# A three-block window-attention kernel: input turning and table preparation in one stage, parameter loads on two queues

## What is computed

```python
xn   = layernorm(x) * g1 + b1
q, k, v = split(window_partition(roll(xn)) @ qkv_w + qkv_b)
attn = softmax(q @ k.T * 8**-0.5 + rel_table[rel_index] + shift_mask)
x    = x + roll_back(window_reverse(attn @ v @ proj_w + proj_b))
x    = x + gelu((layernorm(x) * g2 + b2) @ w1 + c1) @ w2 + c2
```

## Time and profile before

| what | value |
|---|---|
| median of three runs | 7142.31 us (7137.75 to 7150.61) |
| profiled execution | 7153.04 us, of it 7151.3 us span |
| PE, DVE, ACT, POOL busy over the span | 96%, 46%, 63%, 31% |
| last `evac_cm` of the input turning | 175.0 us |
| DVE starts to clear `V3` | 317.9 us |
| DMA share of the first and last fortieth of the span | 8 and 7 tenths, 0 between |

### The profile page before, as it was taken

How to read it: one execution, slowest core, us unless ns; L and a number is a source line. 1 busy time by engine, 2 the same in 40 slices (tenths; PEclk the granted TensorE clock), 3 DMA queues, 4 the chain that set the end, 5 groups by cost and what they waited for, 6 DMA issues and landing times.

```text
span 7151.3 us, 325290 instructions
## 1 busy us (share of the span) xinstructions
PE 6879.3 (96%) x141786; PEld 4832.6 (68%) x141786; DVE 3312.7 (46%) x6694; ACT 4473.2 (63%) x6933; POOL 2233.0 (31%) x2070
## 2 busy tenths in 40 slices
PE   6599999999999999999999999999999999999997
PEld 4277676777677777776777677777776777677764
DVE  6444444444444444444444444444444444444444
ACT  0166666666666666666666666666666666666660
POOL 4033333333333333333333333333333333333330
PEclk9699999999999999999999999999999999999995
DMA  8000000000000000000000000000000000000007
GB/s 246 22 19 24 23 25 23 23 24 23 23 24 23 23 24 23 25 23 23 25 23 24 24 23 24 24 23 25 23 25 23 23 25 23 23 23 25 23 19 236
DMA packets 291287, 244.34 MB, mean 34 GB/s; under 512 B 45888, under 2 KB 285474, under 8 KB 289570
## 3 DMA queue, kind: packets, MB, share of 16 engines
q1 hardware_dynamic: 245238, 180.65, 9.4%
q10 hardware_dynamic: 36414, 19.95, 0.9%
q0 software_dynamic: 8192, 22.49, 0.9%
HBM read 113.42 MB, written 109.53 MB: 31 GB/s over the span
## 4 chain that ended last, share of the span: by engine, by line
PE 93%; DMA 3%; issue 2%; DVE 1%; SPq 0%; POOL 0%; ACT 0%; POOLq 0%; DVEq 0%; ACTq 0%
PE pS L959 14%; PE pA L1001 14%; PE pS L972 9%; PE pA L922 7%; PE pB L1010 6%; PE pS L981 6%; PE pB L1058 5%; PE pA L1050 5%; PE pB L1041 4%; PE pB L1079 4%; PE pB L1098 4%; PE pA L928 4%; PE pA L1089 3%; PE pB L1018 3%; PE pB L1106 3%; PE pA L1018 2%
## 5 line engine op out<-in xcount | busy, mean ns | idle before, releaser
L461 POOL TENSOR_TENSOR Kbd<-KT,headmask 128x588 f32<-128x588 f32 x768 | 895.5, 1166 | 3358.1 <-DVE KT L740 3358.1
L729 DVE TENSOR_REDUCE mx<-pS 113x12 f32<-113x588 f32 x1536 | 1181.0, 769 | 1259.2 <-PE pS L981 1253.5
L959 PE MATMUL pS<-bias,stackr 128*128 128x296 f32 x6096 | 1334.6, 341 | 3.6 <-ACT E L531 3.3
L531 ACT ACTIVATE E<-pS 113x588 f32<-113x588 f32 x1536 | 1004.8, 654 | 451.2 <-DVE mx L729 420.3
L461 POOL TENSOR_TENSOR Qbd<-Qt,headmask 128x588 f32<-128x588 f32 x768 | 895.9, 1167 | 1068.6 <-DVE Qt L734 1068.6
L959 PEld LDWEIGHTS pS<-bias,stackr 128*128 128x128 f32 x6096 | 932.3, 189 | 328.3 <-issue 227.3
L1001 PEld LDWEIGHTS pA<-E,V 113*54 113x54 f32 x36864 | 962.0, 131 | 112.3 <-issue 111.9
L1001 PE MATMUL pA<-E,V 113*54 113x49 f32 x36864 | 1010.8, 215 | 1.1 <-ACT va L520 0.8
L515 ACT ACTIVATE sq<-pB 112x392 f32<-112x392 f32 x768 | 381.8, 497 | 789.7 <-PE pB L1010 789.7
L972 PE MATMUL pS<-Kbd,Qt 24*49 24x147 f32 x24576 | 765.7, 304 | 0.0
L981 PE MATMUL pS<-Qbd,KT 27*49 27x147 f32 x24576 | 707.0, 285 | 0.0
(11 more groups left out here) (126 smaller groups left out, 9085.4 us busy)
## 6 DMA issues: line engine op xcount, KB each, us to landing
xin<-xT SPq DMA_DIRECT2D x384, 98.0 KB, 2.0
xT<-xout SPq DMA_DIRECT2D x384, 98.0 KB, 1.9
xin<-xT SPq DMA_DIRECT2D x384, 73.5 KB, 2.0
xT<-xout SPq DMA_DIRECT2D x384, 73.5 KB, 1.8
xT<-cm POOLq DMA_DIRECT2D x128, 171.5 KB, 3.7
cm<-xT SPq DMA_DIRECT2D x128, 171.5 KB, 3.4
tm<-in_x SPq DMA_DIRECT2D x128, 147.0 KB
out<-tm ACTq DMA_DIRECT2D x128, 147.0 KB
```

What stands on the lines that cost most here:

```text
L461: return pool.tensor_tensor(y, x, m, ALU.mult)
L531: act.activation(e, s, ACT.Exp).then_inc(exp_done, 1)
L729: dve.tensor_reduce(m, s, AX.X, ALU.max).then_inc(mx_done, 1)
L959: mm(pS[:, q, S1:S1 + 2 * SW], stackr[:, :], rows, start=True, stop=False)
```

## The change

On every engine the 128 turning steps are now written out, without loops. On DVE and PE a counter `turned` and two helpers, `turn(n)` and `turn_to(step)`, place them between the instructions of the preparation:

- DVE: one step behind each of the three one-hot instructions, behind each pair of `neg`, behind each group of six mask additions, behind `high`, behind each `bias` pair, and behind the scaling of each block's weights. The waits for `whole` stand at step 48 (block 0), 90 (block 1) and 100 (block 2). The second index's one-hot tiles are made at step 32, before the first `bias`.
- PE: the first gather begins at step 10 with one step behind each matmul (20 matmuls, steps 10 to 30), the second at step 38 with two steps behind each (steps 38 to 78). The bias matmuls come at step 110, the centring at the end. The centring uses banks 2, 3 and 7 in place of 0, 1 and 2.
- Queues: ACT loads the six table pieces first (a semaphore of their own, `tab_in`), then 28 parameters. It now issues the store of `gath` and the loads of `whole`. Another 28 parameters are issued by ACT between the second store of `gath` and the wait for it. The other 97 parameters are issued by SP, one behind each tile load from step 4 on. SP loads the second index behind the tile of step 20.
- POOL: the same 128 stores, written out.

The core of the diff:

```diff
+        BY_ACT = 56
 (SP)
             load_index(0)
-            for c in range(4, UN):
+            sp.wait_ge(zeroed, len(CLEARED) + 1)
+            for c in range(4, STEPS):
                 load_x(Step(0, c))
-            with sp.Fori(1, STEPS // UN) as u:
...
+                if c - 4 < len(par) - BY_ACT:
+                    to, of = par[BY_ACT + c - 4]
+                    sp.dma_start(to, of).then_inc(par_in, 16)
+                if c == 20:
+                    sp.wait_ge(onehot, 1)
+                    load_index(1)
 (ACT)
-            for to, of in par:
+            for to, of in tabs:
+                act.dma_start(to, of).then_inc(tab_in, 16)
+            for to, of in par[0:BY_ACT // 2]:
                 act.dma_start(to, of).then_inc(par_in, 16)
...
+                act.wait_ge(gat_done, 10 * (k + 1))
+                act.dma_start(gat[k, 0:kept], gath[rows]).then_inc(gat_out, 16)
+                if k:
+                    for to, of in par[BY_ACT // 2:BY_ACT]:
+                        act.dma_start(to, of).then_inc(par_in, 16)
+                act.wait_ge(gat_out, 16 * (k + 1))
+                for t in ts_:
+                    if t:
+                        act.wait_ge(whole_used, t)
...
 (DVE)
+            def turn_to(step):
+                while turned[0] < min(step, STEPS):
+                    c = turned[0]
+                    spread_x(Step(0, c))
+                    if c:
+                        evac_cm(Step(0, c - 1))
+                    turned[0] += 1
...
+            turn(4)
+            one_hot(0)
...
+            turn_to(32)
+            one_hot(1)
             for k, (_, ts_) in enumerate(TABLES):
...
                 for t in ts_:
+                    turn_to((48, 90, 100)[t])
                     dve.wait_ge(whole_in, 128 * (t + 1))
...
 (PE)
+            turn_to(10)
+            pe.wait_ge(tab_in, 16 * len(tabs))
...
+                turn_to((10, 38)[k])
                 pe.wait_ge(onehot, k + 1)
...
                         mm(o, tab[:, 0, heads], ..., start=True, stop=False)
+                        turn(1 + k)
                         mm(o, tab[:, 1, heads], ..., start=False, stop=True).then_inc(gat_mm, 1)
+                        turn(1 + k)
+            turn_to(110)
+            pe.wait_ge(par_in, 16 * len(par))
```

More of the change, by code:

```diff
@@ L204, in build @@
         const_in = sem("const_in")
-        par_in = sem("par_in")
+        par_in, tab_in = sem("par_in"), sem("tab_in")
         idx_in = sem("idx_in")
@@ L629, in evac_cm, with turn, one_hot @@
                 dve.tensor_copy(strided(cm[:, b, 0:1], [[TK, TP], [1, TK]]), src).then_inc(cm_done, 1)
-            dve.wait_ge(zeroed, 1)
[L632 to L640, removed]
+            turned = [0]
+            def turn_to(step):
[5 more added lines that the diff above has]
+                    turned[0] += 1
+            def turn(n=1):
+                turn_to(turned[0] + n)
+            def one_hot(k):
+                dve.wait_ge(idx_in, 16 * (k + 1))
+                chain(dve.tensor_copy(idx_f[:, :], idx_i[:, :]))
+                turn()
+                if k:
+                    dve.wait_ge(gat_mm, 10)
+                dve.tensor_scalar(oh_lo[:, :], idx_f[:, :], kcol[:, 0:1], None, ALU.is_equal)
+                turn()
+                dve.tensor_scalar(oh_hi[:, :], idx_f[:, :], kcol[:, 1:2], None, ALU.is_equal).then_inc(onehot, 1)
+                turn()
+            dve.wait_ge(zeroed, 1)
+            turn(4)
             dve.wait_ge(zeroed, len(CLEARED) + 1)
@@ L868, in transpose_x, with turn_to, turn @@
                 last.then_inc(tr_done, 1)
-            for c in range(UN):
-                transpose_x(Step(0, c))
-            with pe.Fori(1, STEPS // UN) as u:
-                for c in range(UN):
-                    transpose_x(Step(u, c))
-            pe.wait_ge(cm_done, STEPS)
-            pe.wait_ge(par_in, 16 * len(par))
+            turned = [0]
+            def turn_to(step):
+                while turned[0] < min(step, STEPS):
+                    transpose_x(Step(0, turned[0]))
+                    turned[0] += 1
+            def turn(n=1):
+                turn_to(turned[0] + n)
+            turn_to(10)
+            pe.wait_ge(tab_in, 16 * len(tabs))
+            pe.wait_ge(zeroed, len(CLEARED) + 1)
             g = 0
             for k, (_, ts_) in enumerate(TABLES):
+                turn_to((10, 38)[k])
                 pe.wait_ge(onehot, k + 1)
```

59 lines of the change are left out of this document (24 added, 35 removed).

## The result

| | before | after |
|---|---|---|
| median of four runs each | 7140.78 us (7137.75 to 7150.61) | 7061.51 us (7058.22 to 7062.18) |
| ratio, 95% interval | | 0.9886 (0.9869 to 0.9903) |
| last turning copy (`evac_cm`) starts | 175.0 us | 228.1 us |
| DVE starts to clear `V3` | 317.9 us | 239.0 us |
| from there to the first copy of the output turning | 6682.0 us | 6669.0 us |

The kernel is 79.3 us faster by the medians. The forecast was 77 us and 7065 us. The head alone is shorter by 78.9 us. The two profiled executions differ by 92 us, and the other 13 us lie in the pipeline, whose code is the same. They belong for the most part to the profiled execution of before: in the twelve experiments the pipeline, whose code is the same in all, took 6664 to 6677 us.

The account below looks back on a forecast made before the run. PE bounds the pipeline, which stays unchanged; only the head can move. Terms of +54.7 us on the turning put the clearing of `V3` at 240.7 us instead of 317.9, 77 us less: 7065 us, range 7050 to 7081.

Parts of the forecast that it names:

- The range: Whole kernel: gain of 61 to 92 us from the bounds of single terms; total 7050 to 7081 us, elsewhere 7085.
- The ring of stores: Turning of the input: a ring of four `cm` buffers takes 5.2 us, which sets 1.30 us a step.
- I put it at zero: Turning loops written out on every engine: takes some register instructions away, counted as no gain.
- Step 3: First gather, turning steps 10 to 30, PE sets the pace: 40 us against 26, +14 us (+10 to +24).
- Steps 6 and 10: Masks, `high` and `bias` of blocks 0 and 2, turning steps 48 to 65 and 100 to 117: +10.3 us each.
- Step 7: Turning steps 65 to 77, PE sets the pace: 1.57 us a step, +3.2 us (0 to 5).
- Step 8: New DVE wait for `whole` at turning step 90, behind 28 parameter issues on ACT: +3.6 us (0 to 8).
- Step 11: Bias matmuls at PE's turning step 110, where DVE sets the pace: +1 us (0 to 3).
- Held tile loads: Rival: parameter loads in SP's queue hold the tile loads behind them; 17 us slower, 7159 us, chance 0.04.
- Slow gathers: Rival: in the gathers PE stays at 1.2 GHz and strided passes double to 1.74 us; 7110 us, chance 0.16.
- Full cover: Rival: the turning catches up at once, DVE's own work is the floor; gain 118 us, 7024 us, chance 0.14.
- Starved stores: Rival: woven DVE instructions make POOL's stores of `cm` 3.5 us late; +9.5 us, 7075 us, chance 0.08.

Follow-up runs that it names:

- e3: The kernel before with the 128 turning steps written out on SP, DVE, PE and POOL, nothing woven: 7132.47 us, ratio 0.9988.
- e11: The kernel before with the 128 turning steps written out on SP, DVE, PE and POOL, run once more: 7135.10 us, ratio 0.9986.
- e5: The changed kernel with ACT's second 28 parameter loads moved behind block 1's loads of `whole`: clearing of `V3` at 236.1 us, 2.9 us earlier.
- e2: The kernel before with only the division of the loads, 97 of them on SP behind tile loads, nothing woven: 7140.47 us, ratio 1.000.
- e6: The changed kernel with the second index loaded in seven pieces behind tile loads 16 to 22: clearing of `V3` at 237.1 us, 1.9 us earlier.

## Why the prediction was right, and where it was not

The sum came within 2 us of the head (78.9 against 77), but by terms that erred both ways. The mechanism held, each stretch as long as its slowest engine or wait makes it; that the number came so close is in part luck. In the sum block 0's stretch was 3.7 us too long and the second gather's 3.5, the way to `high` of block 1 was 5.8 us too short and the bias matmuls 2.2.

- **What bounds the kernel.** Right. Nothing behind the clearing of `V3` changed.
- **The range.** Its bounds were added up wrongly. With all the bounds named at one end together, the gain is 54 to 98 us, not 61 to 92. The measured 78.9 lies in both. The upper end of the total also reads 7081 us in one place and 7085 in another.
- **The ring of stores.** Right as the pace of the plain turning. But 1.30 us a step was the pace of the looped turning; written out it is 1.23 and 1.22 (`e3`, `e11`). "I put it at zero" is the one term that failed outright: it is worth 9 to 10 us when the turning is not woven. What of it is in the 79 us is open.
- **Step 3, the first gather.** 40 us forecast, 40.0 measured, by two errors. `way` 0 went faster, since PE, without a gap, stays at the higher clock (14.8 us against 17). In `way` 1, "the load of the second index hides" was wrong: it held stores for 5.1 us and a tile for 1.1 us.
- **Steps 6 and 10, `bias`.** Mechanism right, DVE full. The size was off: 28.7 us against 32.4, because the turning's two copies overlap and cost 0.74 us, not 0.92. Counting mean durations of back-to-back instructions counts the overlap twice. The rows had shown it: from 9.4 to 177.2 us DVE is busy 108.24 us, while 128 steps of 0.92 us make 118. The prediction's DVE share of 170 us up to 318 us is such a sum too; the busy time of that window is 161 us. In step 10 the 3.2 us of step 11 filled the gap.
- **Step 7.** 15.3 us against 18.8: PE was full, at the higher clock, two steps in 2.64 us.
- **Step 8, the new wait.** Right in place and cause (`e5` removes it), 6.2 us against 3.6, inside its bounds. The 28 issues took 16.6 us, with one pair of 3.6 us among them. The turning steps ahead of it also took 3.2 us more than the sum has, for stores that came late.
- **Step 11.** 3.2 us against 1, just beyond the bound of 3: the matmuls stood at the lower clock, and DVE was not far enough ahead.
- **Held tile loads.** Refuted by `e2`. Its sign, DVE waiting for `tm`, did appear after the change, with 2.2 us in all once the turning runs, 1.06 of it behind the index load; before the change it was 3.5 us. **Slow gathers**: refuted by the rows of 1.83 us at both levels of the clock. **Full cover**: refuted; PE and DVE each had windows without a gap.
- **Starved stores.** Half right. POOL's timeline after the change:

```profile
18.57 1.20 POOL L436 DMA_DIRECT2D xT<-cm  x1 [3.98 <-DVE cm L634]
...
231.94 0.52 POOL L436 DMA_DIRECT2D xT<-cm  x1 [3.33 <-issue]
```

Under `oh_lo` and `oh_hi`, under the second `idx_f` and under `high` of blocks 0 and 2, a store's issue takes 1.12 to 1.20 us instead of 0.53: seven of the 128. Each of the seven ends 0.11 or 0.12 us behind the DVE instruction it ran under. That is at most 0.67 us of a ring that has room for it, and the lock that the Trainium skill describes ("SBUF — State Buffer", "Who interferes with whom") agrees in kind: the delay stays within the one DVE instruction. But the row on which the rival rested was misread. After the change the last store is 3.33 us late again, while DVE runs nothing from 228.6 to 231.3 us; it was 3.2 to 3.6 us late in all fourteen profiles, those in which DVE had one-hot tiles to make and those in which it had not. The late last store is not DVE's doing. What it is stays open.

## What to carry to other kernels

Work that is woven into a bandwidth-bound loop is hidden only as far as each engine's room in a step goes; add it up step by step per engine, take the pitch from starts and not from mean durations, and expect the bound to change hands. When work moves, look at what is queued behind each transfer issue on its new engine: here, in the woven kernel, 46 of 79 us hung on ACT's copies not standing behind small loads. Weave only what does not form a chain of its own across the two engines that pass the loop's work to each other, or each link costs a full step.

## What the runs showed of the hardware

- A moving operand read with a step of 49 float32 columns takes 0.87 us a pass for 490 columns, and two such passes take 1.83 us at a granted clock of 0.54 and of 1.00 alike; a plain pass takes 0.41 us at 2.4 GHz and 0.82 at 1.2 GHz.
- The granted clock reads 1.00 in the looped turning, while its matmuls last as long as those in stretches with 0.50. Where the two disagree, this document reads the level from the durations; no run separates the two.
- One broadcast load to 128 partitions of 2401 columns (1200.5 KB, 9.4 us to its landing) holds other transfers: stores that land in 3.3 us (median) took up to 9.1 us, and in seven pieces the longest wait fell from 5.1 to 2.8 us (`e6`).
- A store that POOL issues while DVE runs a cast or `tensor_scalar` over 2368 or 2401 float32 columns takes 1.12 to 1.20 us to issue instead of 0.53.
- The last store of a row of stores on POOL's queue starts 3.2 to 3.6 us late in all fourteen profiles, whatever DVE does.
